# Last feed-forward of a two-block AdaLN network: another order of the low-part steps, the projections and the norm steps

## The reference, cut to what matters

```python
def _L1_ffn_ref(x, w1_w, w1_s, w2_w, w2_s, h1_w, h1_s, h2_w, h2_s, w3_w, w3_s):
    def _tlin(x, w, s):
        return jnp.einsum('bsi,oi->bso', x, w) * s      # weights are -1, 0, 1
    h = jax.nn.silu(_tlin(x, w1_w, w1_s)) * _tlin(x, w2_w, w2_s)   # 128 -> 512
    h = jax.nn.gelu(_tlin(h, h1_w, h1_s), approximate=False)        # 512 -> 512
    h = jax.nn.gelu(_tlin(h, h2_w, h2_s), approximate=False)        # 512 -> 512
    return _tlin(h, w3_w, w3_s)                                     # 512 -> 128
...
    h = _layernorm(x, axis=-1) * (1 + cb) + sb
    x = x + gb * _L1_ffn_ref(h, ...)
```

## Time and profile before

| | us |
|---|---|
| median of three runs | 1004.08 |
| the profiled execution's own time | 1001.47 |
| its span | 1000.2 |
| the last feed-forward's first matmul | at 810.03 |
| its last instruction on an engine (GpSimd's last addition) | 996.60 to 997.86 |

### The profile page before, as it was taken

How to read it: one execution, slowest core, us unless ns; L and a number is a source line. 1 busy time by engine, 2 the same in 40 slices (tenths; PEclk the granted TensorE clock), 3 DMA queues, 4 the chain that set the end, 5 groups by cost and what they waited for, 6 DMA issues and landing times.

```text
span 1000.2 us, 25506 instructions
## 1 busy us (share of the span) xinstructions
PE 857.0 (86%) x9999; PEld 527.1 (53%) x9999; DVE 732.9 (73%) x1794; ACT 656.5 (66%) x1154; POOL 407.3 (41%) x667
## 2 busy tenths in 40 slices
PE   5688888876463799999999999999999759798997
PEld 3344455554342466666666666666666524443444
DVE  4776888888794787778787877778788366666654
ACT  4668888854442466767675676766676648585865
POOL 3043555446565565573655547364132210101001
PEclk9889999999786599999999999999999989999999
DMA  5000000000142252626335262633642000000000
GB/s 154 22 1 1 1 1 0 1 1 1 54 122 66 83 145 70 176 52 173 86 100 127 69 180 48 168 91 98 181 121 52 3 0 1 22 1 22 1 23 22
DMA packets 70698, 63.60 MB, mean 64 GB/s; under 512 B 30600, under 2 KB 62824, under 8 KB 70576
## 3 DMA queue, kind: packets, MB, share of 16 engines
q1 hardware_dynamic: 70064, 61.90, 23.4%
q10 hardware_dynamic: 512, 0.02, 0.0%
HBM read 34.02 MB, written 27.36 MB: 61 GB/s over the span
## 4 chain that ended last, share of the span: by engine, by line
PE 53%; DVE 8%; issue 3%; ACT 3%; POOL 0%; DVEq 0%; POOLq 0%; ACTq 0%
PE bank L2149 12%; PE bank L1727 8%; PE bank L1702 4%; PE bank L1675 4%; PE bank L1683 3%; PE bank L1664 3%; PE bank L1657 2%; PE bank L1667 2%; PE bank L1690 2%; PE bank L1693 2%; PE bank L1735 1%; ACT 4g L2207 1%; DVE bank L1811 1%; DVE 4f L2243 1%; DVE bank L1816 1%
## 5 line engine op out<-in xcount | busy, mean ns | idle before, releaser
L1891 ACT ACTIVATE ET<-bank 64x512 f32<-64x512 f32 x128 | 75.6, 591 | 114.4 <-PE bank L1693 113.3
L1816 DVE TENSOR_TENSOR bank<-bank,WT 128x256 f32<-128x256 f32 x128 | 55.2, 431 | 86.8 <-PE bank L1683 84.7
L2230 DVE TENSOR_TENSOR act<-4f,act 128x512 f16<-128x512 f32 x96 | 66.4, 691 | 57.7 <-ACT act L2197 57.5
L1886 ACT ACTIVATE ET<-bank 128x768 f32<-128x768 f32 x128 | 103.2, 807 | 3.3 <-PE bank L1702 0.9
L1727 PE MATMUL bank<-ET,vv 128*32 128x128 f32 (+2 forms) x1792 | 89.1, 323 | 0.8 <-DVE O L1846 0.8
L1821 DVE TENSOR_REDUCE mo<-bank 128x4 f32<-128x512 f32 x128 | 87.3, 682 | 1.1 <-PE bank L1667 0.9
L2197 ACT ACTIVATE act<-4f 128x512 f16<-128x512 f32 x96 | 60.4, 630 | 28.3 <-DVE 4f L2243 26.2
L1829 DVE TENSOR_REDUCE mo<-bank 128x3 f32<-128x384 f32 x128 | 69.9, 546 | 0.0
L1830 DVE TENSOR_REDUCE mo<-bank 128x3 f32<-128x384 f32 x128 | 69.9, 546 | 0.0
L1811 DVE TENSOR_TENSOR bank<-bank,W 128x256 f32<-128x256 f32 x128 | 54.3, 424 | 12.9 <-PE bank L1657 12.9
L2149 PE MATMUL bank<-act,std 128*128 128x512 f16 x256 | 58.2, 390 | 0.0
(11 more groups left out here) (385 smaller groups left out, 2531.1 us busy)
## 6 DMA issues: line engine op xcount, KB each, us to landing
ring<-scr_q SPq DMA_DIRECT2D x16, 324.0 KB
QO<-scr_q SPq DMA_DIRECT2D x16, 324.0 KB
ring<-scr_a SPq DMA_DIRECT2D x16, 252.0 KB
KA<-scr_a SPq DMA_DIRECT2D x16, 252.0 KB
ring<-scr_k SPq DMA_DIRECT2D x16, 168.0 KB
KB<-scr_k SPq DMA_DIRECT2D x16, 168.0 KB
scr_a<-dk SPq DMA_DIRECT2D x8, 288.0 KB, 4.5
X<-in_x SPq DMA_DIRECT2D x8, 256.0 KB, 5.2
```

Of the source, the lines that this page charges most:

```text
L1816: dve.tensor_tensor(half(psDT, 0), half(psDT, 0), over(WT[:, h * HB:(h + 1) * HB], NT), ALU.mult).then_inc(s_wk, 1)
L1886: act.activation(ET[n % NE][:, T:SEG * P], psXT[:, 0:NP * P], ACT.Exp).then_inc(s_expo, 1)
L1891: act.activation(to[0:HB, :], psDT[0:HB, :], ACT.Exp)
L2230: dve.tensor_tensor(lo, f32_[f % 3], hi, ALU.subtract).then_inc(s_lo, 1)
```

## The change

Four things are changed in this stage. VectorE issues a unit's product in front of the low part of the unit before it, not behind. The projections of a pair, for all pairs but the last, stand inside the next pair's first layer: on TensorE behind the second and the fourth unit, with VectorE's scaling behind the low part that follows the third and the fifth product; the activations of h2 have buffers of their own for that (three layers of them in place of two) and `Y` has two buffers. The last pair's second projection goes to another bank than the first. And the norm's steps no longer stand in the first layer: `step(side, 1 + o % 2)` issues all 24 in h1 and h2, the first sample's in h1, the second's in h2.

```diff
+        def project(pair, s, to):
+            pe.wait_ge(s_lo, split_of(pair, 2, s, NO - 1) + 1)
+            for a in range(NT):
+                m = passes(to[:, a * D:(a + 1) * D], [(rows(act_[s][2], j, a * P, P), [x[:, j * D:(j + 1) * D] for x in wt["w3"]]) for j in range(NO)], False)
+            m.then_inc(s_proj, 1)
...
                     passes(ps[bank_of(pair, k + 1)], [(column(wt["w2"], 0, o), hT[s])]).then_inc(s_up, 1)
-                    step(side)
+                    if pair and k in (2, 6):
+                        p = k // 4
+                        if b - 2 + p:
+                            pe.wait_ge(s_Y, b - 2 + p)
+                        project(pair - 1, p, psY)
...
                         passes(ps[bank_of(pair, k)], [(column(wt[w], j, o), rows(act_[s][l], j)) for j in range(NO)]).then_inc(s_hid, 1)
-                        step(side)
-            for s in range(2):
...
-                m.then_inc(s_proj, 1)
-                step(side, 2)
-            step(side, 24)
+                        step(side, 1 + o % 2)
+        pe.wait_ge(s_Y, B - 2)
+        project(B // 2 - 1, 0, psY)
+        emptied(pe, B // 2, 0)
+        project(B // 2 - 1, 1, ps[bank_of(B // 2, 0)])
...
+        def output(b, at):
+            dve.wait_ge(s_proj, b + 1)
+            if b >= 2:
+                dve.wait_ge(s_add, b - 1)
+            dve.tensor_tensor(tiles(Y[b % 2]), tiles(at), over(sh.row("gb1", b), NT), ALU.mult).then_inc(s_Y, 1)
...
                     n, f = 4 * s + o, split_of(pair, 0, s, o)
-                    if n:
-                        split(pair, 0, (n - 1) // 4, (n - 1) % 4)
                     dve.wait_ge(s_up, 8 * pair + n + 1)
                     dve.wait_ge(s_sil, 8 * pair + n + 1)
...
                     dve.scalar_tensor_tensor(f32_[f % 3], ...).then_inc(s_gated, 1)
-                    step(side)
+                    if n:
+                        split(pair, 0, (n - 1) // 4, (n - 1) % 4)
+                    if pair and n in (2, 4):
+                        output(2 * pair - 2 + n // 2 - 1, psY)
```

More of the change, by code:

```diff
@@ L2196, in split @@
             act.wait_ge(s_gated, 8 * pair + 4 * s + o + 1) if layer == 0 else act.wait_ge(s_gelu, 16 * pair + 8 * (layer - 1) + 4 * s + o + 1)
-            act.activation(act_[s][layer % 2][0][:, o * T:(o + 1) * T], f32_[f % 3], ACT.Copy).then_inc(s_hi, 1)
+            act.activation(act_[s][layer][0][:, o * T:(o + 1) * T], f32_[f % 3], ACT.Copy).then_inc(s_hi, 1)
         for pair in range(B // 2):
@@ L2227, in split @@
             f = split_of(pair, layer, s, o)
-            hi, lo = (x[:, o * T:(o + 1) * T] for x in act_[s][layer % 2])
+            hi, lo = (x[:, o * T:(o + 1) * T] for x in act_[s][layer])
             dve.wait_ge(s_hi, f + 1)
             dve.tensor_tensor(lo, f32_[f % 3], hi, ALU.subtract).then_inc(s_lo, 1)
+        def output(b, at):
[3 more added lines that the diff above has]
+            dve.tensor_tensor(tiles(Y[b % 2]), tiles(at), over(sh.row("gb1", b), NT), ALU.mult).then_inc(s_Y, 1)
         for pair in range(B // 2):
@@ L2249, in on_dve @@
                         split(pair, l + 1, s, o)
[L2250 to L2258, removed]
+                        step(side, 1 + o % 2)
+        output(B - 2, psY)
+        output(B - 1, ps[bank_of(B // 2, 0)])
     def on_pool():
@@ L2266, in on_pool @@
             pool.wait_ge(s_Y, b + 1)
-            pool.tensor_tensor(sh.x(b), sh.x(b), Y[0], ALU.add).then_inc(s_add, 1)
+            pool.tensor_tensor(sh.x(b), sh.x(b), Y[b % 2], ALU.add).then_inc(s_add, 1)
     first_pe, first_dve, first_act = both(normed_pe, 0), both(normed_dve, 0), both(normed_act, 0)
@@ L2275, in main @@
         for i in range(2):
-            act_.append([[c.sb(f"act{i}{l}{x}", NO * T, dt=F16, at=own) for x in range(2)] for l in range(2)])
+            act_.append([[c.sb(f"act{i}{l}{x}", NO * T, dt=F16, at=own) for x in range(2)] for l in range(3)])
+            Y.append(c.sb(f"4Y{i}", T, at=own))
         for i in range(3):
@@ L2279, in main @@
             f32_.append(c.sb(f"4f{i}", T, at=own))
-        Y.append(c.sb("4Y", T, at=own))
         on_sp()
```

## The result

The changed kernel took 1002.16 us (median of 20 runs, 997.75 to 1005.3) and the kernel before 1005.88 (20 runs, 1001.51 to 1008.88). The ratio is 0.9969, with a 95% interval of 0.9956 to 0.9981: 3.1 us faster, where 6.4 were forecast. The direction was right, the size came out at about half, and it is within the 0.5% that I had called no change.

A forecast was written before the change was run, and what follows sets the result against it. TensorE's lost time lay between h2 and the next h1, with products in a 2.05 us ring. Terms -4.5, -11.6, +8.3, -0.7, -2.1, +4.0, +0.2 gave -6.4: 1004.1 to 997.7 us, range 992.5 to 1003.

The forecast's parts named there:

- The swap: Pair 0's first layer: product ahead of low part makes units 1.27 apart, not 2.05; h1 starts near 9.8; -4.5 us.
- Rival 4: First layer: the ring doesn't break, units stay at 2.05 and the new chains build on that; about +12 us; chance 0.05.
- The projections inside the first layer: Three pair boundaries: second projection waits 2.7 us for `Y`, h1 starts at 13.5; -11.6 us.
- The price of GpSimd's addition: Boundaries: VectorE low parts beside GpSimd's addition take some 1.27 us; the second delays VectorE's later chain by 0.6.
- The norm's steps: In h1, TensorE waits 2.0, 2.5 and 2.5 us for `xh`; with transposes formerly in the first layer, +8.3 us.
- The end: Last projection waits only for the last low part, starting 0.73 us after it instead of 1.44; -0.7 us.
- The table load: ScalarE, before the first Silu: now on the path, taking 1.28 us as in the trace, Gelu following at once.
- the rival built on it: ScalarE: each table switch costs double on the path, a second 1.28 us; sum becomes +2.6, 1006.7 us; chance 0.03.
- the clock term: TensorE's clock falls behind half of six new boundary pauses, at 1.3 us each; +4.0 us, bounds none and 10.2.
- falls of before that are gone from h1: h1 of pairs 0 and 2 stays at full clock, saving earlier falls' 1.1 and 1.0 us; -2.1 us.
- the discount: Boundary pauses: a fall behind the first is partly taken back by the second; 1.3 us taken, up to 1.7 possible.
- rival 2: Clock falls at nearly each pause, or the two waits come out a us longer; -2.4 to -0.4 us; chance 0.24.

The follow-up runs named there:

- e5: The kernel before with only VectorE's product moved ahead of the low part; stage 178.3 us, ratio 0.9919 to the kernel before.
- e6: The changed kernel with VectorE's product behind the low part again; stage 208.0 us, ratio 1.0208 to the kernel before.
- e4: The changed kernel with unread matmuls put into TensorE's waits for `Y` and `xh`; stage 178.0 us, ratio 0.9899 to the kernel before.
- e1: The changed kernel with each pair's second projection in psT, the transposes' bank; stage 174.3 us, ratio 0.9862 to the kernel before.
- e2: The changed kernel with TensorE's four transposes of a sample two steps later; stage 177.4 us, ratio 0.9911 to the kernel before.
- e7: The kernel before with product ahead of low part and norm's steps in h1 and h2, projections behind h2; stage 177.5 us, ratio 0.9916 to the kernel before.

## Why the prediction was right in its parts and wrong in size

**The swap** was right: units at 1.26 (1.27), h1 of pair 0 at 9.9 (9.8). e5 shows that it alone gives more than the whole change, e6 that the other parts without it cost 20 us of stage. Rival 4, which is e6's mechanism, had been priced at +12. **The projections inside the first layer** were right: a wait of 2.63 (2.7), and h1 13.7 us after the pair's first matmul (853.29 to 866.99; 13.5). **The price of GpSimd's addition** was right, 1.32 for the low part beside it (1.27). **The norm's steps** were right: waits of 1.64, 2.41 and 2.41 (2.0, 2.5, 2.5). **The end** too: the last projection starts 0.84 after the last low part (992.06 to 992.90; 0.73), in place of 1.44. **The table load** took what the trace had shown: in the changed kernel it starts at 855.38 and the first Silu at 856.67. The 1.28 for the load in the Trainium skill (ScalarE: Activation LUTs, "What ACT_TABLE_LOAD costs") agrees with that; its longer figure, 2.66 with the drain, finds no room there, and the rival built on it is out. On ScalarE:

```profile
855.38 1.28 ACT L2212 ACT_TABLE_LOAD   x1
856.67 1.27 ACT L2212 ACTIVATE 4g<-bank,roots 128x512 f32<-128x512 f32 x2
```

**The step that failed is the clock term**, "I take half of six, at 1.3: +4.0". There were four falls, and they cost nearly all that a fall can: 5.30 against 3.62 for 16 matmuls of h1, twice, and 3.68 and 3.49 against 2.16 for a second projection. That is 1.68 + 1.68 + 1.52 + 1.33 = 6.2 in place of 4.0, and e4, which takes away the falls and leaves the waits to end when they did, brings 6.2. Both factors were short: four falls for three, 1.55 for 1.3.

The stage came out 2.8 above its forecast (187.8 - 6.4 = 181.4, measured 184.2). Term by term, in us; a boundary runs from the end of h2 (853.29, 899.80 and 947.83 after) to the next h1 (866.99, 915.01, 962.85), which makes 13.7 each without the two falls of 1.52 and 1.33:

| term | forecast | measured |
|---|---|---|
| first layer of pair 0 | -4.5 | -4.35 |
| three boundaries, without falls | -11.6 | -10.9 |
| norm's steps in h1 and h2, with restarts | +8.3 + 0.2 | +8.35 |
| the end | -0.7 | -0.6 |
| falls of before that are gone from h1 | -2.1 | -2.3 |
| new falls | +4.0 | +6.2 |
| sum | -6.4 | -3.6 |

2.2 of the 2.8 are the clock term; the largest of the others is the 0.2 by which h1 starts later than worked out at each of three boundaries (13.7 for 13.5). From h1 to h1 the changed kernel took 44.1, 48.0 and 47.8 us where before took 46.6, 45.9 and 46.0: behind pair 0's first layer it lost some 1.5 us up to the last h1, where the prediction had it win a little at each boundary.

The reason I gave for the discount, that a fall behind the first pause is partly taken back by the second "which hangs on VectorE", was wrong: the wait for `xh` stayed at 2.41 behind the projection of 3.68. VectorE's chain hangs itself on the gate matmuls of unit 4, which stand behind that projection, so the fall moves both: the transposes of that h1 start 28.15 after the pair's first matmul (899.80 to 927.95), a boundary without a fall has 26.63 (853.29 to 879.92), and the 1.52 between them is the whole of what the fall cost the projection.

The measured ratio, -3.1 us over 20 runs a side, agrees with the stage's -3.6. Of rival 2 the first half, "the clock falls at nearly each pause", came nearest, with four of six; its band began at -2.4, and the truth lies between it and the forecast. The count of falls is that of one execution: three or five would have fitted the same mechanism. How often the clock falls behind such a wait in other executions than the profiled ones is open.

## What to carry to other kernels

When an edit shortens a ring on a helper engine and also regroups TensorE's work, price the two apart, and look for where the pauses go: here a wait of 1.7 and two or three pauses of 1 us a boundary became a wait of 2.6 and mostly another of 2.4, with four falls of the clock where there had been three, and that was no gain. A wait in the middle of dense matmuls costs its own length and, when the clock fell, cost another 1.3 to 1.7 us here; and if it is a wait for a single bank or for a chain that starts late, a bank idle in that phase and a later place in the row are the cure. A check costs little: put matmuls that nobody reads into the wait and see whether the kernel gets faster.

## What the runs showed of the hardware

- Filling TensorE's waits with matmuls whose result is not used made the stage 6.2 us shorter (e4): the waits ended when they had, and the four falls of the clock were gone.
- Falls differ at like waits: of the changed kernel's three waits of 2.63 one had none, of e1's two of 2.9 one, while e2's three of 2.63 had one each. Of the three waits of 1.7 in e5, and of those in e7, one each had a fall; in the kernel before, none of three.
- At waits of about 4 us (e6) the clock was at half for 6.8 us, 1.1 to 1.8 of it before the wait was over; at those of 2.4 to 2.9 it was for 3.4, or not at all.
- A VectorE subtraction of two SBUF operands took 1.32 in place of 0.68 beside a GpSimd addition of 1.27 that had started 0.5 before it.
